# Rotary attention: the value matmuls behind the transposes and in three pieces, V in zero-filled blocks

## The reference, cut to what matters

```python
B, T, C = x.shape                      # 4, 512, 256
H = NUM_HEADS                          # 16
D = C // H                             # 16
qkv = x @ w_atten.T
q, k, v = jnp.split(qkv, 3, axis=2)    # then (B, H, T, D)
q = apply_rope(q, rope)
k = apply_rope(k, rope)
att = jnp.einsum('bhqd,bhkd->bhqk', q, k) * (1.0 / jnp.sqrt(jnp.float32(D)))
att = jnp.where(causal[None, None], att, jnp.float32(-jnp.inf))
att = jax.nn.softmax(att, axis=-1)
y = jnp.einsum('bhqk,bhkd->bhqd', att, v)
y = y.transpose(0, 2, 1, 3).reshape(B, T, C)
return y @ w_proj.T
```

## Time and profile before

| | |
|---|---|
| median of 3 runs | 4483.51 us (4479.13 to 4487.49) |
| profiled execution | 4471.5 us, span 4469.8 us |
| busy over the span | PE 3423.8, PEld 2730.5, DVE 2825.6, ACT 2225.1, POOL 1804.9 us |
| the stage's first instruction | 957.86 us |
| the next stage's first instruction | 1525.50 us |

### The profile page before, as it was taken

The page is one execution under the profiler, slowest core; times in us unless marked ns, Lnnn a source line. Parts: engine busy times, 40 slices in busy tenths (PEclk is TensorE's granted clock), DMA queues, the critical chain, the costliest instruction groups (busy, mean ns, idle before and its releaser), DMA issues. The chain is left out here.

```text
span 4469.8 us, 73441 instructions
## 1 busy us (share of the span) xinstructions
PE 3423.8 (77%) x20792; PEld 2730.5 (61%) x20795; DVE 2825.6 (63%) x6109; ACT 2225.1 (50%) x5849; POOL 1804.9 (40%) x3124
## 2 busy tenths in 40 slices
PE   7799939716776549449999999999464799999364
PEld 3355637515665437338878788787353688888353
DVE  5799766635555466458858678587352667667452
ACT  3699604316566314148868678587011444444111
POOL 0499615575443025536536355364155000000155
PEclk9799959859999769769999999999666899999566
DMA  2111134420000314420000000000524100000524
GB/s 78 27 47 48 31 133 125 124 64 1 1 1 1 127 37 140 110 72 19 19 10 19 14 16 19 9 19 19 166 41 89 48 2 1 1 1 1 167 42 102
DMA packets 133291, 222.64 MB, mean 50 GB/s; under 512 B 28624, under 2 KB 106448, under 8 KB 131104
## 3 DMA queue, kind: packets, MB, share of 16 engines
q1 hardware_dynamic: 99184, 148.95, 9.9%
q0 software_dynamic: 33792, 69.83, 7.0%
HBM read 163.71 MB, written 54.80 MB: 49 GB/s over the span
## 5 line engine op out<-in xcount | busy, mean ns | idle before, releaser
L1256 POOL DMA_INDIRECT ex_xr<-scratch_rows,mo_token x288 | 287.1, 997 | 348.2 <-issue 311.8
L598 POOL TENSOR_TENSOR sc_h<-sc_h,sc_c 128x512 f32<-128x512 f32 x256 | 327.3, 1293 | 196.6 <-DVE sc_h L635 188.8
L3199 DVE TENSOR_TENSOR sa_pT<-bank,sa_pT 128x512 fp32r<-128x512 f32 x512 | 329.9, 686 | 34.2 <-ACT sa_pT L3067 30.3
L3059 ACT ACTIVATE sa_p<-bank,sa_nm 128x512 f32<-128x512 f32 x512 | 346.9, 689 | 2.5 <-DVE sa_nm L3190 2.5
L635 DVE TENSOR_TENSOR_SCAN sc_h<-sc_da,bank 128x512 f32<-128x512 f32 x256 | 311.1, 1220 | 38.0 <-ACT sc_da L578 23.1
L2888 PE MATMUL bank<-sa_kT,sa_qT 128*128 128x512 f32 x1024 | 332.5, 436 | 1.5 <-DVE residual L3166 1.5
L3186 DVE TENSOR_REDUCE sa_mx<-bank 128x2 f32<-128x1024 f32 x256 | 312.4, 1220 | 25.7 <-PE bank L2890 21.9
L1322 PE MATMUL bank<-mo_w_gu,ex_xT 128*128 (+2 forms) x1152 | 312.7, 400 | 3.0 <-ACT ex_xT L1370 2.5
L2912 PE MATMUL bank<-sa_pT,sa_v 128*128 128x256 f32 x2048 | 301.5, 290 | 17.0 <-DVE sa_pT L3199 16.5
L1370 ACT ACTIVATE ex_xT<-bank 128x256 f32<-128x256 f32 (+1 forms) x288 | 105.5, 366 | 409.1 <-PE bank L1304 384.4
L2912 PEld LDWEIGHTS bank<-sa_pT,sa_v 128*128 128x128 f32 x2048 | 260.2, 190 | 40.2 <-DVE sa_pT L3199 32.0
(11 more groups left out here) (380 smaller groups left out, 9705.2 us busy)
## 6 DMA issues: line engine op xcount, KB each, us to landing
scratch_ys<-ex_yo SPq DMA_DIRECT2D x192, 128.0 KB
mo_w_gu<-in_w_gu SPq DMA_DIRECT2D x2, 9216.0 KB, 27.0
sc_c<-scratch_c SPq DMA_DIRECT2D x64, 256.0 KB, 3.1
sa_share<-scratch_shares SPq DMA_DIRECT2D x256, 64.0 KB, 2.6
mo_w_dn<-in_w_dn SPq DMA_DIRECT2D x2, 4608.0 KB, 48.1
mo_w_dn<-in_w_dn SPq DMA_DIRECT2D x2, 4096.0 KB, 33.6
scratch_rows<-ln_stage POOLq DMA_DIRECT2D x64, 128.0 KB, 4.9
ex_xr<-scratch_rows,mo_token POOLq DMA_INDIRECT x288
```

The source lines that it names most:

```text
L598: pool.tensor_tensor(h, h, C[u], ALU.mult).then_inc(used.sem, 1)
L1256: pool.indirect_dma_start(xr[u][:, :], None, rows, bass.IndirectOffsetOnAxis(ap=token[:, i:i + 1], axis=0), bounds_check=rows.shape[0] - 1 ...
L3059: act.activation(pr[h][:, :], SC[2 * s_ + h][:, :], ACT.Exp, bias=nm[:, col:col + 1], scale=SCALE, accum_out=rs[:, col:col + 1]).then_inc( ...
L3199: dve.tensor_tensor(spot(1), PT[h][:, :].rearrange("p (k n) -> p k n", k=TPB), spot(0).bitcast(F32), ALU.subtract).then_inc(*inc("kept_d"))
```

## The change

The value matmuls of head M are issued at N = 4M + 7 (the block of keys 0), 4M + 8 (block 1) and 4M + 9 (blocks 2 and 3), each behind that iteration's `turn_p`, which now follows directly on the score. The other work comes behind them. `pT` has three pairs of buffers instead of two.

V lies in blocks of 128 columns for each head and each 128 keys, filled with zeros once by POOL; only the head's own 32 columns are written afterwards. The four heads of a group add into the bank `OB` without being cleared between them, and `keep_parts` copies all 128 rows once a group, at unit 6 of the next group. `turn_parts` and `normalize` move from r = 4 to r = 8, `turn_qk` to r = 4 to 7, and output product and its transposes some units later.

`qT` has no zeros any more: two heads lie in rows 0 to 63 and 64 to 127, as in `kT`, ACT writes both with one instruction, and a score contracts over 64 rows. The projection of group 1 comes behind the turning of group 0's q and k. On ACT the other copies follow `high_p` and `expo` instead of preceding them.

```diff
-        vv = [sb(f"v{u}", [P, TPB * HG * 2 * D], F32R) for u in range(4)]
-        qT = [sb(f"qT{u}", [P, HG * SEQ], F32R) for u in range(2)]
+        VW, VS = HG * P, P + 2 * D
+        vv = [sb(f"v{u}", [P, TPB * VW + P], F32R) for u in range(4)]
+        qT = [sb(f"qT{u}", [P, HG // 2 * SEQ], F32R) for u in range(2)]
...
-        pT = [[sb(f"pT{u}_{w}", [P, TPB * SEQ], F32R) for w in range(2)] for u in range(2)]
+        pT = [[sb(f"pT{u}_{w}", [P, TPB * SEQ], F32R) for w in range(2)] for u in range(3)]
...
+        def v_parts(I, i):
+            return vv[I % 4][:, i * VW:i * VW + HG * VS].rearrange("p (h e) -> p h e", h=HG)[:, :, 0:2 * D] \
+                .rearrange("p h (s d) -> p h s d", s=2)
...
-                for u in range(2):
-                    for hh in range(HG):
-                        rows = slice(WR, P) if hh % 2 == 0 else slice(0, WR)
-                        pool.wait_ge(*at("made", 4 + u * HG + hh))
-                        pool.memset(qT[u][rows, hh * SEQ:(hh + 1) * SEQ].bitcast(F32), 0.0).then_inc(*inc("made"))
-                pool.wait_ge(*at("made", 4 + 2 * HG))
+                for u in range(4):
+                    pool.memset(vv[u][:, :].bitcast(F32), 0.0).then_inc(*inc("made"))
+                pool.wait_ge(*at("made", 8))
...
-                    pe.matmul(bank[:, 0:keys(qt)], qT[I % 2][:, hh * SEQ + qt * P:hh * SEQ + (qt + 1) * P],
-                              kT[I % 2][:, hh // 2 * SEQ:hh // 2 * SEQ + keys(qt)], start=True, stop=False)
+                    rows = slice(hh % 2 * WR, (hh % 2 + 1) * WR)
+                    pe.matmul(bank[:, 0:keys(qt)], qT[I % 2][rows, hh // 2 * SEQ + qt * P:hh // 2 * SEQ + (qt + 1) * P],
+                              kT[I % 2][rows, hh // 2 * SEQ:hh // 2 * SEQ + keys(qt)], start=True, stop=False)
...
-                def values(M):
-                    I = M // HG
-                    pe.wait_ge(*at("kept_d", M * TPB + TPB))
-                    if M % HG == 0:
-                        pe.wait_ge(*at("klow", (I + 1) * TPB))
-                    if M >= 1:
-                        pe.wait_ge(*at("ylow", M))
-                    for kb in range(TPB):
+                def values(M, blocks):
+                    I, hh = divmod(M, HG)
+                    if blocks[0] == 0:
+                        pe.wait_ge(*at("kept_d", M * TPB + TPB))
+                        if hh == 0:
+                            pe.wait_ge(*at("klow", (I + 1) * TPB))
+                            if I >= 1:
+                                pe.wait_ge(*at("ylow", I))
+                    for kb in blocks:
                         for w in range(2):
-                            last = pe.matmul(OB[:, kb * P:SEQ], vv[I % 4][:, kb * P:(kb + 1) * P],
-                                             pT[M % 2][w][:, kb * SEQ + kb * P:(kb + 1) * SEQ],
-                                             start=(kb == 0 and w == 0), stop=(kb == TPB - 1 and w == 1))
-                    last.then_inc(*inc("summed"))
+                            last = pe.matmul(OB[:, kb * P:SEQ], vv[I % 4][:, kb * VW + hh * P:kb * VW + (hh + 1) * P],
+                                             pT[M % 3][w][:, kb * SEQ + kb * P:(kb + 1) * SEQ],
+                                             start=(hh == 0 and kb == 0 and w == 0),
+                                             stop=(hh == HG - 1 and kb == TPB - 1 and w == 1))
+                    if blocks[-1] == TPB - 1:
+                        last.then_inc(*inc("summed"))
...
-                for I in range(2):
-                    for i in range(TPB):
-                        project(I, i)
+                for i in range(TPB):
+                    project(0, i)
                 for j in range(TPB):
                     turn_qk(0, j)
+                for i in range(TPB):
+                    project(1, i)
...
-                    if N >= 6 and (N - 6) % TPB == 0 and (N - 6) // TPB < NH:
-                        values((N - 6) // TPB)
-                    if r < TPB and I + 2 < NG:
+                    if 2 <= N < NU + 2:
+                        turn_p(N - 2)
+                    if 0 <= M < NH and piece < 3:
+                        values(M, ((0,), (1,), (2, 3))[piece])
+                    if r < 4 and I + 2 < NG:
                         project(I + 2, r)
...
-                        for half in range(2):
-                            rows = slice(half * WR, (half + 1) * WR)
-                            last = act.activation(qT[I % 2][rows, (2 * m + half) * SEQ:(2 * m + half + 1) * SEQ],
-                                                  bank[rows, :], ACT.Copy, scale=SCALE)
+                        last = act.activation(qT[I % 2][:, m * SEQ:(m + 1) * SEQ], bank[:, :], ACT.Copy, scale=SCALE)
...
-                def keep_parts(M):
-                    I, hh = divmod(M, HG)
-                    rows = slice(hh * 2 * D, (hh + 1) * 2 * D)
-                    dve.wait_ge(*at("summed", M + 1))
-                    if I >= 2 and hh == 0:
+                def keep_parts(I):
+                    dve.wait_ge(*at("summed", (I + 1) * HG))
+                    if I >= 2:
                         dve.wait_ge(*at("yturned", I - 1))
-                    dve.tensor_copy(yq[I % 2][rows, :], OB[rows, :]).then_inc(*inc("ylow"))
+                    dve.tensor_copy(yq[I % 2][:, :], OB[:, :]).then_inc(*inc("ylow"))
...
+                    if 2 <= N < NU + 2:
+                        low_p(N - 2)
+                    if N >= UNITS + 6 and (N - 6) % UNITS == 0:
+                        keep_parts((N - 6) // UNITS - 1)
-                    if r < TPB and I + 2 < NG:
+                    if r < 4 and I + 2 < NG:
                         low_v(I + 2, r)
-                    if r == 4 and I >= 1:
+                    if r == 8 and I >= 1:
                         normalize(I - 1)
```

More of the change, by code:

```diff
@@ L2329, in _ @@
                             put(I + 2, i)
-                        if i == 1 and I >= 1:
-                            add_parts(I - 1)
+                    if I >= 1:
+                        add_parts(I - 1)
             @block.tensor
@@ L2427, in product @@
                     last.then_inc(*inc("outp"))
-                pe.wait_ge(*at("made", 4 + 2 * HG))
+                pe.wait_ge(*at("made", 4))
                 for i in range(TPB):
@@ L2476, in fetch @@
                        .then_inc(*inc("qraw"))
-                    if I >= 4 and i == 0:
+                    if I < 4 and i == 0:
+                        act.wait_ge(*at("made", 4 + I + 1))
+                    elif i == 0:
                         act.wait_ge(*at("summed", (I - 3) * HG))
-                    act.activation(vv[I % 4][:, i * P:(i + 1) * P].rearrange("p (h s d) -> p h s d", s=2, d=D)[:, :, 0, :],
+                    act.activation(v_parts(I, i)[:, :, 0, :],
                                    spare("p", I, i)[:, 2 * QW:CW].rearrange("p (h d) -> p h d", d=D), ACT.Copy) \
@@ L2521, in _ @@
                     keep_x(0, i)
-                for I in range(2):
-                    for i in range(TPB):
-                        fetch(I, i)
+                for i in range(TPB):
+                    fetch(0, i)
                 for j in range(TPB):
                     keep_qk(0, j)
+                for i in range(TPB):
+                    fetch(1, i)
                 for N in range(NU + UNITS):
-                    I, r = divmod(N, UNITS)
-                    if r < TPB and I + 2 < NG:
-                        fetch(I + 2, r)
-                    if 5 <= r < 9 and I + 1 < NG:
-                        keep_qk(I + 1, r - 5)
-                    if 9 <= r < 13 and I % G == 1 and I // G + 1 < BATCH:
-                        keep_x(I // G + 1, r - 9)
-                    if 8 <= r < 12 and I % G == 0 and I >= 1:
-                        keep_y(I // G - 1, r - 8)
                     if 2 <= N < NU + 2:
@@ L2540, in _ @@
                         expo(N)
+                    I, r = divmod(N, UNITS)
+                    if r < 4 and I + 2 < NG:
+                        fetch(I + 2, r)
+                    if 4 <= r < 8 and I + 1 < NG:
+                        keep_qk(I + 1, r - 4)
+                    if 9 <= r < 13 and I % G == 1 and I // G + 1 < BATCH:
+                        keep_x(I // G + 1, r - 9)
+                    if 10 <= r < 14 and I % G == 0 and I >= 1:
+                        keep_y(I // G - 1, r - 10)
             @block.vector
@@ L2568, in low_v @@
                 def low_v(I, i):
-                    both = vv[I % 4][:, i * P:(i + 1) * P].rearrange("p (h s d) -> p h s d", s=2, d=D)
+                    both = v_parts(I, i)
                     dve.wait_ge(*at("vput", I * TPB + i + 1))
@@ L2631, in _ @@
                         stand(I // G + 1, r - 7)
[L2632 to L2637 removed]
+                    if 12 <= r < 16 and I % G == 0 and I >= 1:
+                        add_out(I // G - 1, r - 12)
         for n, v in dict(
[L2640 removed]
```

(2 more changed lines are left out.)

68 lines of the change are left out of this document (30 added, 38 removed).

## The result

The changed kernel takes 4342.85 us (median of 4 runs, 4340.68 to 4350.06), the kernel before 4483.58 in the same rounds (4479.13 to 4487.49). The ratio is 0.9689, 95% interval 0.9672 to 0.9706: 139 us less (132 to 147). The new kernel's profiled execution took 4350.06 us, its slowest run; its span is 4348.3 us. The stage runs from 959.54 to 1408.60 us, 449.1 us against 567.6 in the trace of before.

The account below looks back on a forecast made before the run. The stage was taken as bound by waits between engines, none of them full. 15 groups at 6.5 us less (98) and 4 from the start made 102 us, off the median 4483.5: 4382 us, range 4345 to 4445.

Parts of the forecast that it names:

- Layer norm, output product and low clock are kept as they cost now: Group length: these three stay at 1.6 us in each group of four heads.
- the 12 us between profiled execution and median: Median 4483.5 against profiled 4471.5 us: taken as unrelated to the changed stage, so the saving came off the median unchanged.
- Rival 4: Engines fill up better: heads at 4.0 us, no collisions, low clock gone, a group of 22.2, 4336 us; chance 0.12.
- The value wait (101.4 us) goes: PE's value matmuls, moved behind the transposes, find DVE's low part ready, so their whole 101.4 us wait goes.
- rival 3: The wait moves to the transposes, waiting for the exponential; half of the 102 us comes back, 4433 us; chance 0.18.
- A plain head at 4.2 us: A head without projection or turning of q and k takes 4.2 us, from hand-stepped instruction starts, where it took 6.63.
- 64-row scores at nothing: Changing PE to 64 rows and back, 512 changes, bounded at 0 to 123 us, was taken as costing nothing.
- rivals 1 and 2: Drains at 64-row scores: partly hidden, 0.12 us a change, 4443, chance 0.10; paid in full, 0.24 us, 4505, chance 0.05.
- A group of 25.3 us: Four heads 16.8, PE extras 4.5, ACT and DVE collisions 2, bank wait 0.4, rest 1.6: 25.3 against 31.8 us.
- The shared bank "inside the 4.2": 64 copies of y on DVE become 16, 33 us less work, already inside the 4.2 us head and not counted again.
- Zero fill and copies: POOL's fill 9.7 us, hidden; 16 copies of y at 0.684 us; 32 copies of q at about 0.599 us.
- The start, 8 regained and 4 lost: At the stage's start, with group 1 projected behind group 0's turning: 4 us lost to POOL, 8 regained.

Follow-up runs that it names:

- before_filled: The kernel before with four unused 512-column matmuls on PE ahead of the values' wait for DVE: 4450.3 us, ratio 0.9917.
- the three filled kernels: before_filled, before_64_filled, and the changed kernel with values in one block at their old place and three zero-adding matmuls ahead of their wait (4409.4 us).
- full_rows: The changed kernel with q in zero-filled places of 128 rows again, so scores use all rows and q takes two copies: 4346.5 us, ratio 0.9704.
- before_64_filled: The kernel before with 64-row scores, one q copy for two heads, and four unused matmuls ahead of the value wait: 4442.5 us, ratio 0.9908.
- two_copies: The changed kernel with ACT's one copy of q for two heads written as two of 64 rows: 4346.3 us, ratio 0.9711.
- plain_start: The changed kernel with both groups projected ahead of the first transposes of q and k, as before: 4339.3 us, ratio 0.9668.
- copy_per_head: The changed kernel without the shared bank: V packed as before and y copied once a head, 64 copies: 4403.2 us, ratio 0.9827.
- before_again: The kernel before, unchanged, traced a second time: 4487.2 us in one run, stage 580.6 us.

## Why the prediction missed, point by point

**The step that failed** is "Layer norm, output product and low clock are kept as they cost now", and with it the sentence that the 12 us between profiled execution and median "have nothing to do with it". So what the change would win in clock was put at nothing. The 139 us are 102 for the change of order at a held clock (0.9917 − 0.9689, uncertain by 10) and 37 for the clock (31 to 43). The stages of the traces say the same: 98 us from before_filled to the changed kernel, and 20 and 33 from the two traces of before to before_filled. The forecast was 102.

The 12 us did bear on it: the second execution of before that was traced is longer than the first by 15.7 us, and 12.6 of them are heads at a lower clock. Against the first trace alone the changed kernel's traced execution gained 121 us (4471.5 to 4350.1). The 19 us up to the medians' difference are the 12 of before and 7 by which the changed kernel's own traced execution lay above its median.

The change closed the waits of the value matmuls (1.17 to 2.25 us in the earlier trace rows) behind which the clock was seen to fall, and the three filled kernels show that closing those waits holds it: from 0.93 and 0.89 to 0.99, from 0.85 to 1.00, from 0.84 to 0.97. Rival 4 named the low clock, priced at 1.6 us a group with its neighbours, and gave it a chance of 0.12; its time, 4336, is the nearest. But its heads of 4.0 us were not what happened.

**The value wait (101.4 us) goes.** Right: one of 1.1 us is left, and the transposes did not take it over (0.9 us; rival 3 is out).

**A plain head at 4.2 us.** The loop was right (4.18 in full_rows), the length is 4.40, since the 64-row form makes PE the bound.

**64-row scores at nothing.** The price exists, 0.67 us a head of PE's busy time, 0.17 a score. From the start of a score to that of its mask it is less: 0.36 us for 384 columns (1386.57 to 1386.93), where the kernel before took 0.26 (1248.65 to 1248.91). The kernel pays nothing for it in sum (full_rows, before_64_filled). That ACT's saved copies give it back fits the third head of full_rows; two_copies shows it only in part. So the term was right in the time and wrong in its reason, "no more than its usual spacing": the sign is the 43.1 and 28.2 us of idle weight loads, and gaps of 0.1 us or more at the scores were the prediction's own sign for rivals 1 and 2. The gaps came and the rivals' times, 4443 and 4505, did not: 0.67 us a head is 0.08 us of PE's busy time for each of eight changes, against their 0.12 and 0.24, and the kernel's time did not grow by it. The Trainium skill's rule ("TensorEngine Tiling (Array Packing)", Key Properties: a change of tiling mode drains the engine) agrees with the gaps ahead of the score's weights (43.1 us in 190 times, 0.23 each).

**A group of 25.3 us.** It was 23.9 (61 heads from 1027.36 to 1391.82, 5.97 each). By its terms: heads 17.6 for 16.8; extras 5.0 for 4.5 (22.59 − 4 × 4.40); collisions of ACT and DVE about nothing for 2, because PE in its order covers them all (22.59 of 22.77 busy); the bank's new wait 0.2 for 0.4; layer norm, output and low clock 1.1 for 1.6. The collisions are the term that was furthest off, 30 us over 15 groups, and heads and extras took 20 of them back. Since the sum priced the 64-row form at nothing, full_rows is the kernel that it described, and there its terms come out closer: heads 16.7 (4 × 4.18), extras 4.4 (19.30 − 4 × 3.73), and 1.8 left of the 22.88 for collisions and bank, where the forecast had 2.4. The form then fills PE over these gaps. The 31.8 us of before hold some clock as well: at the held clock it is 30.6 a group (482.58 / 63 × 4). So without the clock the difference is 6.7 a group, where the prediction had 31.8 − 25.3 = 6.5. Both of its lengths were too long, the first by 1.2 us and the second by 1.4, and the errors cancelled. That the forecast's 102 us meet the 102 (or 98) of the order alone is luck.

**The shared bank "inside the 4.2".** Right as far as it went, but one wait was left unpriced: with late values and a copy for each head, PE waits for DVE in most heads, and the kernel is 60 us slower, a part of it by the clock.

**Zero fill and copies.** 7.46 us for 9.7, hidden; 16 copies of 0.682; 32 of 0.590. As said.

**The start, 8 regained and 4 lost.** The wait for POOL came, 4.70 us at 1006 to 1011. The first value of the third head comes 67.8 us after the stage's start for 67.1 before, so nothing was regained in sum. The 8 us themselves are real: with the order of before (plain_start) that value comes at 59.2. The term that was mis-sized is the loss, 8.6 us for 4: the projection of group 1 left a wait of 12.23 us and now lies behind it.

**What remains open.** How much each part of the change keeps of the clock isn't separated, least of all in copy_per_head. The costs of leaving out one part (65 us for the place, some 20 for the pieces, 60 for the shared bank) add up to more than the 102 of the order; that each part needs the others is likely, and not shown. All traces are of single executions.

## What to carry to other kernels

Where PE waits again and again, as here 1.2 to 2.3 us in every head, and its mean clock is below 1.00, price the wait twice: once as time on the chain, once as clock. Filling the wait with unused matmuls measured the second alone here (the warm group kept its 30.25 us), and told which experiments were disturbed by it. Take two traces of the kernel before when the clock varies; a difference between the profiled execution and the median may lie in the very stage that is to be changed. Move work off the end of a chain together with the buffer that it then meets: here the late values without the shared bank gave away 60 of 139 us, clock included. And look for what fills a wait already: the projections that were moved out of the start's wait cost 8.6 us.

## What the runs showed of the hardware

Unused work made a kernel faster: 256 matmuls more, 37 us less. A score on 64 rows between instructions on 128 keeps PE busy 0.17 us longer, with the weight loads of score and mask idle for 0.22 us each (71.3 us in 319 times) on no other engine. A group of the same instructions takes 30.25 us at a clock of 1.00 and 33.41 at 0.85, and PE idles for 10 and 9 us of them. The changed kernel, too, lost its clock in places, in a group that PE all but filled:

```profile
1110.36:1140.54 30.18, 28.85 (x164) 21.22 (x165) 18.50 (x45) 20.64 (x65) 14.77 (x42) 0.94 0.00 1
```

It carries an output product beside its heads and is long for that reason as well. What PE did where the clock fell is the same as in before_again, with a single wait:

```profile
1112.01 0.59 PE L2404 MATMUL bank<-ra_pT,ra_v 128*128 128x384 f32 x2
...
1116.17 0.44 PE L2423 MATMUL bank<-ident,ra_y 128*128 128x128 f32 x2 [1.16 <-POOL ra_y L2321]
...
1119.24 0.99 PE L2404 MATMUL bank<-ra_pT,ra_v 128*128 128x384 f32 x2
```

PE had waited 1.16 us for POOL's sum of the output parts, and behind that the same two value matmuls took 0.99 us instead of 0.59. From 1118.26 to 1121.76 the granted clock was 0.59, and 1.00 from there on. The next such wait, 1.14 us up to 1216.19, was followed by 0.50 from 1218 to 1220. A third of 1.14 us, up to 1316.16, was followed by 1.00, so such a wait goes ahead of the fall but doesn't settle it. The kernel before had no such wait between its first and last head; whether the later `add_parts` makes it wasn't tried.
